# Decoder layer with a routed expert stage: expert results added to the output in memory instead of stored, read back and weighted

## The chip, the cores and the metric

The kernel runs on one core of one Trainium2 chip. The metric is the device time of one execution in microseconds (us). The engines of a core are TensorE (PE), VectorE (DVE), ScalarE (ACT), GpSimd (POOL) and SyncE (SP); 16 DMA engines move data, at the word of SP's queue and of POOL's.

## What is computed

A decoder layer on x of shape 4 x 512 x 512: grouped-query attention, a gated state-space mixer, and a feed-forward part with experts. Only the last matters here:

```
topk_indices, topk_weights = _router(x, router_weight, e_bias)      # 2 of 16 experts per token, weights sum to 1
combine = zeros((T, 16)).at[arange(T)[:, None], topk_indices].add(topk_weights)
h1 = einsum('th,ehi->tei', x, w_up)
a = relu2(h1) * combine[:, :, None]                                  # relu2(v) = relu(v)**2
routed = einsum('tei,eih->th', a, w_down)
shared = relu2(hidden_states @ shared_up) @ shared_down
x = x + routed + shared                                              # hidden_states is the normalized x
```

There are 2048 tokens, so 4096 pairs of a token and an expert. w_up of an expert is 512 x 256, w_down 256 x 512, all in float32.

## The kernel before

All stages stand in one program. Attention and the scan of the mixer take the first 660 us or so. Then `close` (from line 1332) runs the normalizations, the shared feed-forward part and the router; `tiles` (from line 1902) runs the routed experts and ends the kernel. The order of work on each engine is written out by hand, and every engine waits on semaphores.

**Router.** `Router.choose` (line 1186, on DVE) picks two experts a token and their weights, `count` (1164, PE) and `place` (1258, DVE) give each pair a slot. Slots are sorted by expert, each expert beginning on a multiple of 64, and fill 40 tiles of 128 slots. `inverse` (1298, DVE) builds one-hot matrices in bf16 and two planes of numbers (the high and low part of the token), `collect` (1172, PE) multiplies them in 32 matmuls of 80 columns, and `tokens` (1318, DVE) turns the product into two lists: `token_i` (the token of a slot) and `pair_i` (its row in the scratch array `sorted_y`, twice the token plus the choice; an empty slot gets a row out of bounds, which the store skips). Its last instruction raises `s_routed`. PE reaches `collect` between the shared up-projections of batches 2 and 3 (lines 1666 to 1668). POOL then gathers the first two tiles' rows (lines 1503 to 1505) and goes on squaring hidden values of the last batch; SP loads expert weights as rooms come free (lines 1436 to 1466).

**Loop over 40 tiles.** In step i (functions `step` at lines 2005, 2058 and 2100) PE does the up-projection of tile i (line 2017, 16 float32 matmuls in the two halves of the array), the down-projection of tile i-1 (line 2029, 8), two transposes of h of tile i (line 2000), and the four transposes of the input of tile i+2 (line 1990, in `turn_x`). ACT copies the down result of tile i-1 out of PSUM into y (line 2065), then h (2068), then the turned input (2054). DVE does relu and square and copies weights for the second half of the array (2080, 2085). POOL's list is

```
load(2); load(3)
for i in range(40):
    if i + 4 < 40: load(i + 4)      # waits until PE has turned tile i + 2; indirect gather of 128 rows
    store(i)                        # waits for y(i); indirect scatter into sorted_y, with a bound
```

**End.** PE then does the last 24 down-projections of the shared part of batch 3 (line 2043, 6 of 8 terms for each of 4 banks; the first 2 terms were done ahead at line 1615 and added by DVE at line 1824). When the last scatter has landed, SP reads `sorted_y` back in 16 loads (line 1949) into the rooms of the weights; DVE adds the two results of each token, weighted, to `acc`, the residual sum (32 instructions, line 2124), for batch 3 also the PSUM banks (line 2119); SP writes 16 blocks of `acc` to the output (line 1953).

Of the kernel before, what the change touches and what calls it, by code (L numbers as in the profile page):

```python
# [23 lines left out]
P = 128  # L24
# [1055 lines left out]
class Router:  # L1080
# [3 lines left out]
    def __init__(self, nc, ctx, keep, r, room):  # L1084
# [23 lines left out]
        self.m1 = sb("m1", [P, TT])  # L1108
# [24 lines left out]
        self.index = [room[0][:, n * SLOT_TILES:(n + 1) * SLOT_TILES] for n in range(4)]  # L1133
# [10 lines left out]
    def constants(self, pool):  # L1144
        pool.memset(self.before_bf[:, :], 1.0).then_inc(self.s_const, 1)
        pool.wait_ge(self.s_const, 1)

        pool.affine_select(out=self.before_bf[:, :], in_=self.before_bf[:, :], compare_op=ALU.is_ge, fill=0.0, base=-1,
                           pattern=[[1, P]], channel_multiplier=-1).then_inc(self.s_const, 1)
        pool.memset(self.ones_bf[:, :], 1.0).then_inc(self.s_const, 1)  # L1150
        pool.memset(self.ones[:, :], 1.0).then_inc(self.s_const, 1)
        pool.memset(self.base[:, 0, :], 0.0).then_inc(self.s_const, 1)
        for out, pattern, first, per_partition in (
                (self.falling, [[-1, E]], E, 0), (self.unit_start, [[HALF, B * T // HALF]], 0, 0), (self.unit_id, [[1, UNIT_SLOTS]], 0, 0),
                (self.row_id, [[1, P]], 0, 0), (self.tile_row, [[P, SLOT_TILES + 1]], 0, 0),
                (self.token_hi, [[0, 2], [1, B * NT]], 1, 0), (self.token_lo, [[P, 2], [0, B * NT]], 0, 1)):
            pool.iota(out[:, :], pattern, base=first, channel_multiplier=per_partition,
                      allow_small_or_imprecise_dtypes=True).then_inc(self.s_const, 1)
# [13 lines left out]
    def collect(self, pe, out):  # L1172

        pe.wait_ge(self.s_inverse, 1)
        for n in range(2 * B * NT):
            last = pe.matmul(out[:, 0:2 * SLOT_TILES], self.in_row[:, n, :], self.planes[:, n, :, :].rearrange("p w i -> p (w i)"),
                             start=(n == 0), stop=(n == 2 * B * NT - 1))
        last.then_inc(self.s_token, 1)
# [7 lines left out]
    def choose(self, dve):  # L1186
# [52 lines left out]
        for k in range(2):  # L1239

            link(dve.tensor_reduce(m1[:, :], score[:, :, :], AX.X, ALU.max))
            tt(tmp[:, :, :], score[:, :, :], per_tile(m1[:, :]), ALU.is_equal)
            tt(tmp[:, :, :], tmp[:, :, :], per_expert(falling[:, :]), ALU.mult)
            link(dve.tensor_reduce(m1[:, :], tmp[:, :, :], AX.X, ALU.max))
            tt(hot[k], tmp[:, :, :], per_tile(m1[:, :]), ALU.is_equal)
# [10 lines left out]
        dve.tensor_tensor(count_bf[:, :].rearrange("p (t e) -> p t e", e=E), hot[0], hot[1], ALU.add).then_inc(self.s_count, 1)  # L1256

# [40 lines left out]
    def inverse(self, dve):  # L1298
# [15 lines left out]
        for w, token in enumerate((self.token_hi, self.token_lo)):  # L1314
            self.link(dve, dve.tensor_tensor(self.planes[:, :, w, :], self.in_tile[:, :, :], over(token[:, :], NI), ALU.mult))
        dve.tensor_tensor(self.in_row, over(self.row[:, :], P), each(self.row_id[:, :], P), ALU.is_equal).then_inc(self.s_inverse, 1)

    def tokens(self, dve, psum):
        dve.wait_ge(self.s_token, 1)
        hi, lo = psum[:, 0:SLOT_TILES], psum[:, SLOT_TILES:2 * SLOT_TILES]  # L1320
        choice, token, pair, none = self.index
        self.link(dve, dve.tensor_scalar(choice, lo, float(P), None, ALU.is_ge))
        self.link(dve, dve.tensor_scalar(token, hi, float(P), -float(P), ALU.mult, ALU.add))
        self.link(dve, dve.scalar_tensor_tensor(pair, choice, -float(P), lo, ALU.mult, ALU.add))
        self.link(dve, dve.tensor_tensor(token, token, pair, ALU.add))
        self.link(dve, dve.scalar_tensor_tensor(pair, token, 2.0, choice, ALU.mult, ALU.add))
        self.link(dve, dve.tensor_scalar(none, token, 0.0, float(4 * B * T), ALU.is_lt, ALU.mult))
        self.link(dve, dve.tensor_scalar(self.r["token_i"][:, :], token, 0.0, None, ALU.max))
        dve.tensor_tensor(self.r["pair_i"][:, :], pair, none, ALU.add).then_inc(self.r["s_routed"], 1)


def close(nc, d, keep, r):

    ctx = ExitStack()
    with ctx:
# [68 lines left out]

        routed = tiles(nc, d, keep, ctx, r, bank, dve_base, pool_sq, pe_down)
# [3 lines left out]
        def _(sp):  # L1409
# [39 lines left out]
            expert(8)  # L1449
            sp.wait_ge(pe_down.sem, pe_down.upto(4 * 2 - 1))  # L1450
# [3 lines left out]
            expert(11)  # L1454
            sp.wait_ge(r["s_routed"], 1)
# [10 lines left out]
            expert_down(10)  # L1466
            routed["sync"](sp)

        @block.gpsimd
        def _(pool):  # L1470
# [32 lines left out]
            for i in range(2):  # L1503
                pool.indirect_dma_start(out=r["x_first"][:, i, :], out_offset=None, in_=d["norm_rows"],
# [7 lines left out]
        def _(pe):  # L1512
# [88 lines left out]
            def turn_first():  # L1601
                pe.wait_ge(act_relu.sem, act_relu.upto(FK * B - 1))
                pe.wait_ge(r["s_x"][0], 16)
                for k in four:
                    last = pe.transpose(bank[0][:, k * P:(k + 1) * P], r["x_first"][:, 0, k * P:(k + 1) * P], ident[:, :])
# [273 lines left out]
def experts(nc, d, keep):  # L1879

    ctx = ExitStack()
    with ctx:
# [6 lines left out]
            "pair_i": sb([P, SLOT_TILES], U32),  # L1889
# [3 lines left out]
            "x_first": sb([P, 2, D]),  # L1893
            "late": sb([P, LATE]),
            "room": sb,
            "s_x": [ctx.enter_context(nc.semaphore(f"e_x{s}")) for s in range(2)],
# [5 lines left out]
def tiles(nc, d, keep, ctx, r, bank, dve_base, pool_sq, pe_down):  # L1902
# [3 lines left out]
    TT = B * NT  # L1906
    UP = KD * FE

    x_in = [r["x_first"][:, 0, :], r["x_first"][:, 1, :]]
# [6 lines left out]
    y = [keep["attn"][:, 0, s * D:(s + 1) * D] for s in range(2)]  # L1916
    halves = [slice(0, HALF), slice(HALF, P)]

    back = [r["w_all"][:, t, 0:2 * D] for t in range(TT)]
    s_x = r["s_x"]  # L1920
    s_y = [ctx.enter_context(nc.semaphore(f"e_y{s}")) for s in range(2)]
    s_g = [ctx.enter_context(nc.semaphore(f"e_g{s}")) for s in range(TT - 2)] + [keep["s_x"][b].sem for b in (1, 2)]
    before = [0] * (TT - 2) + [keep["s_x"][b].upto(NT) for b in (1, 2)]
    s_o = ctx.enter_context(nc.semaphore("e_out"))
# [10 lines left out]
    pair = Track(nc, ctx, "e_pair", ["first", "second"], 2)  # L1935
    s_late_out, s_late_add = keep["s_late_out"], keep["s_late_add"]
# [8 lines left out]
    def sync(sp):  # L1945
        sp.wait_ge(s_y[0], 16 * (LAST // 2 + 1))
        sp.wait_ge(s_y[1], 16 * ((LAST + 1) // 2))
        for t in range(TT):
            sp.dma_start(back[t], d["sorted_y"][2 * t * P:2 * (t + 1) * P, :].rearrange("(p k) c -> p (k c)", k=2)).then_inc(s_g[t], 16)
        with sp.Fori(0, B) as b:  # L1950
            for t in range(NT):
                pair.wait(sp, b * NT + t, "second")
                sp.dma_start(d["out"][b, t * P:(t + 1) * P, :], keep["acc"][:, b, t * D:(t + 1) * D]).then_inc(s_o, 16)
        sp.wait_ge(s_o, 16 * TT)

    def gpsimd(pool):
# [6 lines left out]
        def store(i):  # L1963
            act_l.wait(pool, i, "y")
            pool.indirect_dma_start(out=d["sorted_y"][0:2 * B * T, :], in_=y[i % 2], in_offset=None, bounds_check=2 * B * T - 1, oob_is_err=False,  # L1965
                                    out_offset=bass.IndirectOffsetOnAxis(ap=r["pair_i"][:, i:i + 1], axis=0))\
                .then_inc(s_y[i % 2], 16)

        load(2)
        load(3)  # L1970
        for i in range(SLOT_TILES):
            if i + 4 < SLOT_TILES:
                load(i + 4)
            store(i)
# [71 lines left out]
    def scalar(act):  # L2046
# [24 lines left out]
        run(step)  # L2071

# [21 lines left out]
    def vector(dve):  # L2094
        dve_m.start(dve)
        pair.start(dve)
# [16 lines left out]

        for t in range(TT):
            dve.wait_ge(s_g[t], before[t] + 16)
            acc = keep["acc"][:, t // NT, (t % NT) * D:(t % NT + 1) * D]
            if t // NT == B - 1:
                dve.wait_ge(s_late_out.sem, s_late_out.upto(t % NT))
                dve.tensor_tensor(acc, bank[t % NT][:, :], acc, ALU.add).then_inc(s_late_add.sem, s_late_add.tick(t % NT))
                dve.wait_ge(s_late_add.sem, s_late_add.upto(t % NT))  # L2120
            for k in range(2):
                if k == 1:
                    pair.wait(dve, t, "first")
                pair.done(dve.scalar_tensor_tensor(acc, back[t][:, k * D:(k + 1) * D], r["weight"][k][:, t:t + 1], acc, ALU.mult, ALU.add),
                          ("first", "second")[k])
# [4 lines left out]
def decoder_layer(nc, d):  # L2130
    with ExitStack() as ctx:
# [21 lines left out]
        keep["s_late_out"], keep["s_late_add"] = Signal(nc, ctx, "late_out"), Signal(nc, ctx, "late_add")  # L2153
# [61 lines left out]
```

## Time and profile before

| | us |
|---|---|
| median of 3 executions (1126.65 to 1132.16) | 1128.84 |
| profiled execution, its time | 1128.89 |
| profiled execution, its span | 1127.2 |
| PE busy in the span | 1060.9 |
| DVE busy | 845.7 |
| POOL busy | 656.7 |

The span runs from the first to the last instruction; the time of the same execution is 1.7 us more. The profile's rows give the start of an instruction or merged group from the span's start, its duration, engine, line of the kernel, operation, what it writes and reads, and in brackets how long the engine had been idle before it and what ended that. The chain of waits follows back from the last instruction what released each step. The windows view sums busy time of each engine in a stretch and gives the granted clock of PE: 1.00 is 2.4 GHz, 0.50 is 1.2 GHz, and a value between them means that part of the stretch ran at either.

### The profile page before, as it was taken

What the parts mean: (1) busy time and instruction counts of PE and PEld (TensorE: products, weight loads), DVE (VectorE), ACT (ScalarE), POOL (GpSimd) and SP (SyncE); (2) the same over time, 40 slices, a digit from 0 to 9 for tenths busy, and PEclk for the clock granted to TensorE, in tenths of its full rate; (3) what the DMA queues carried; (4) which work ended last, traced back from release to release, by engine and by line L of the source; (5) the groups of instructions that cost most, each with busy time, mean ns of one, the idle gap of its engine ahead of it and who ended that gap; (6) DMA issues with size and microseconds to landing.
All of it is one profiled execution on the core that took longest, in us unless ns stands there. A gap on an engine that the chain in (4) does not pass through costs nothing.

```text
span 1127.2 us, 19610 instructions
## 1 busy us (share of the span) xinstructions
PE 1060.9 (94%) x6786; PEld 620.4 (55%) x6786; DVE 845.7 (75%) x1297; ACT 676.8 (60%) x1492; POOL 656.7 (58%) x573
## 2 busy tenths in 40 slices
PE   8999988888999999999989889999999999999993
PEld 3554556666666667666666654544444445555541
DVE  6988699999999999999999989840680045545548
ACT  4876789999999899999999944412011022333310
POOL 2022299999999999999999955202043024444420
PEclk9999989999999999999999999999999999999997
DMA  7210001102111111010221007112225523333329
GB/s 225 94 39 21 21 29 39 37 31 76 34 34 30 39 67 39 30 38 31 84 75 31 20 23 278 38 74 75 75 75 206 167 81 122 122 112 123 108 76 381
DMA packets 50865, 92.95 MB, mean 82 GB/s; under 512 B 9294, under 2 KB 17486, under 8 KB 50768
## 3 DMA queue, kind: packets, MB, share of 16 engines
q1 hardware_dynamic: 44368, 72.82, 19.4%
q0 software_dynamic: 6400, 18.88, 5.2%
q8 instruction: 56, 0.92, 0.3%
q14 instruction: 41, 0.34, 0.1%
HBM read 72.67 MB, written 19.01 MB: 81 GB/s over the span
## 4 chain that ended last, share of the span: by engine, by line
PE 71%; POOL 8%; DVE 7%; ACT 7%; issue 5%; DMA 1%; SPq 0%; DVEq 0%; ACTq 0%; POOLq 0%
PE ps L1570 10%; PE ps L2017 7%; PE ps L2029 6%; PE ps L843 6%; POOL w_all L765 5%; PE ps L1584 5%; PE ps L871 4%; PE ps L358 4%; PE ps L832 4%; PE ps L817 4%; DVE w_all L1042 3%; PE ps L310 3%; PE ps L1593 2%; ACT w_all L956 2%; PE ps L882 2%
## 5 line engine op out<-in xcount | busy, mean ns | idle before, releaser
L765 POOL TENSOR_TENSOR w_all<-w_all 128x512 f32<-128x512 f32 x256 | 320.7, 1272 | 20.1 <-DVE w_all L587 14.8
L1042 DVE TENSOR_TENSOR_SCAN w_all<-ps,w_all 128x512 f32<-128x512 f32 x256 | 298.6, 1205 | 1.2 <-ACT ps L939 0.6
L939 ACT ACTIVATE ps<-w_all,low 128x512 f32<-128x512 f32 x256 | 177.6, 697 | 1.0 <-DVE w_all L1042 0.8
L871 PE MATMUL ps<-ident,w_all 128*128 128x128 f32 x1024 | 162.0, 281 | 9.7 <-DVE acc L1050 9.5
L947 ACT ACTIVATE w_all<-ps,low 128x128 f32<-128x128 f32 (+3 forms) x256 | 132.8, 530 | 13.6 <-DVE low L1034 13.6
L871 PEld LDWEIGHTS ps<-ident,w_all 128*128 128x128 f32 x1024 | 114.9, 142 | 34.7 <-issue 20.8
L956 ACT ACTIVATE w_all<-ps 128x256 f32<-128x256 f32 (+2 forms) x192 | 101.9, 531 | 22.9 <-PE ps L832 22.6
L1034 DVE TENSOR_REDUCE low<-ps 128x2 f32<-128x256 f32 (+3 forms) x128 | 103.8, 811 | 14.6 <-PE ps L817 13.9
L1570 PE MATMUL ps<-w_all 128*128 128x512 f32 x256 | 112.1, 594 | 0.0
L832 PE MATMUL ps<-ident,w_all 128*128 128x128 f32 x640 | 108.8, 285 | 1.5 <-ACT low L1013 1.5
L843 PE MATMUL ps<-w_all,low 128*32 128x128 f32 x1280 | 95.0, 278 | 12.1 <-ACT w_all L956 10.8
L817 PE MATMUL ps<-w_all,attn 32*128 32x384 f32 (+3 forms) x512 | 105.1, 487 | 0.0
L1497 POOL TENSOR_TENSOR w_all<-w_all 128x512 f32<-128x512 f32 x24 | 32.6, 1362 | 123.8 <-ACT w_all L1704 123.8
L832 PEld LDWEIGHTS ps<-ident,w_all 128*128 128x128 f32 x640 | 70.5, 141 | 51.5 <-issue 48.3
L2065 ACT ACTIVATE attn<-ps 128x512 f32<-128x512 f32 x40 | 24.0, 601 | 121.6 <-PE ps L2029 121.6
L773 POOL TENSOR_TENSOR acc<-acc,low 128x512 f32<-128x512 f32 x64 | 81.7, 1277 | 24.6 <-ACT low L968 24.5
L1965 POOL DMA_INDIRECT sorted_y<-attn,low x40 | 40.6, 1015 | 91.3 <-ACT attn L2065 91.3
L1050 DVE SCALAR_TENSOR_TENSOR acc<-ps,low,acc 128x512 f32<-128x512 f32 x128 | 92.7, 724 | 0.0
L843 PEld LDWEIGHTS ps<-w_all,low 128*32 128x32 f32 x1280 | 60.4, 109 | 46.9 <-ACT w_all L956 24.8
L773 POOL TENSOR_TENSOR acc<-acc,w_all 128x512 f32<-128x512 f32 x64 | 81.9, 1280 | 4.0 <-ACT w_all L968 4.0
L1570 PEld LDWEIGHTS ps<-w_all 128*128 128x128 f32 x256 | 47.8, 190 | 58.5 <-issue 56.8
L2017 PE MATMUL ps<-w_all,attn 128*64 x320 | 79.1, 391 | 0.3 <-issue 0.2
(228 smaller groups left out, 1935.2 us busy)
## 6 DMA issues: line engine op xcount, KB each, us to landing
w_all<-b_scratch SPq DMA_DIRECT2D x64, 256.0 KB, 3.2
w_all<-in_w_up SPq DMA_DIRECT2D x16, 512.0 KB, 6.0
w_all<-in_w_down SPq DMA_DIRECT2D x16, 512.0 KB, 7.1
w_all<-sorted_y SPq DMA_DIRECT2D x16, 512.0 KB, 10.5
norms<-attn SPq DMA_DIRECT2D x4, 1024.0 KB, 4.3
out_dram<-acc SPq DMA_DIRECT2D x16, 256.0 KB, 8.8
attn<-in_x SPq DMA_DIRECT2D x3, 1024.0 KB, 6.0
attn<-in_x SPq DMA_DIRECT2D x12, 256.0 KB, 4.3
```

Of the source, the lines that this page charges most:

```text
L765: pool.tensor_tensor(dbu[:, k, :], keep["du"][i // N][:, k * T:(k + 1) * T], b_all[i % 2][:, :], ALU.mult).then_inc(pool_dbu.sem, pool_dbu ...
L773: pool.tensor_tensor(acc, acc, cy[n % 2][:, :], ALU.add).then_inc(pool_acc.sem, pool_acc.tick(n))
L817: last = pe.matmul(sc[:, x, 0:n], keep["attn"][r:r + DH, b, m * T + j * P:m * T + (j + 1) * P], k_4[r:r + DH, b, m // 2, 0:n], start=False ...
L832: last = pe.transpose(tb[:, at:at + P], prob[:, x, off[j] + t * P:off[j] + (t + 1) * P], ident[:, :])
L843: last = pe.matmul(ob[r:r + DH, j * P:(j + 1) * P], keep["v"][:, b * KV + m // 2, t * DH:(t + 1) * DH], prob_t[unit % 2][:, at:at + P], st ...
L871: last = pe.transpose(yb[which][:, k * P:(k + 1) * P], state[i % 2][:, k, t * P:(t + 1) * P], ident[:, :])
L939: act.activation(da[unit % 2][:, :], keep["dt"][i // N][:, k * T:(k + 1) * T], ACT.Exp, scale=keep["a_flat"][:, unit % (N * KD):unit % (N ...
L947: act.activation(prob[:, x, off[j]:off[j] + n], sc[:, x, 0:n], ACT.Exp, bias=neg_max[unit % 2][:, x:x + 1], accum_out=row_sum[unit // 8 % ...
L956: act.activation(prob_t[unit % 2][:, first * n:(first + heads) * n], tb[:, 0:heads * n], ACT.Copy).then_inc(act_turn.sem, act_turn.tick(tu ...
L1042: dve.tensor_tensor_scan(state[i % 2][:, k, :], da[unit % 2][:, :], dbu[:, k, :], 0.0, ALU.mult, ALU.add).then_inc(dve_scan.sem, dve_scan. ...
L1570: last = pe.matmul(bank[m % 2][:, :], s_up[:, k, m * P:(m + 1) * P], norm_t[b][:, k, :], start=(k == 0), stop=(k == 3))
L2017: last = pe.matmul(bank[2 + s][rows, 0:FE], x_t[s][:, k * P + n * HALF:k * P + (n + 1) * HALF], w, start=(k == 0), stop=(k == KD - 1))
```

## The change

The two results of a token are no longer stored, read back and added by DVE. Instead:

- `choose`, `inverse`, `collect` and `tokens` also carry the weight of each slot (in three bf16 pieces, exact in sum) and whether it is that token's lower or higher expert. The lists are now `token_i`, `first_i` (the output row if this is the lower expert, else out of bounds), `second_i` (the reverse) and `w_slot` (the weight).
- ACT's copy of the down result multiplies each slot's row by its weight. y has 4 buffers (before 2), in `acc` of batch 1.
- SP stores `acc` (residual and shared part) to the output per batch, as soon as it is done: batches 0 and 1 during the shared part, 2 and 3 after the last weights.
- POOL adds y to the output's rows with two accumulating indirect scatters a tile, the second after the first has landed.
- x_in has 4 buffers (before 2), in `acc` of batch 0; four tiles are gathered ahead of the loop.
- The end has no read-backs and no DVE work: ACT copies the four late banks of batch 3, POOL adds them to the output by four accumulating DMAs.

```diff
@@ class Router, choose (after the count is released)
+        for k in range(2):
+            tt(late_half[:, k, :], m1[:, k, :], m1[:, 1 - k, :], ALU.is_lt)
+        link(dve.scalar_tensor_tensor(token_lo, late_half[:, :, :], float(P), token_lo, ALU.mult, ALU.add))
+        for k in range(2):
+            link(dve.tensor_copy(rest[:, k, :], weight[k]))
+        flat = rest[:, :, :].rearrange("p k t -> p (k t)")
+        for w in range(3):
+            link(dve.tensor_copy(piece[:, w, :], flat))
+            if w < 2:
+                tt(flat, flat, piece[:, w, :], ALU.subtract)
@@ inverse
+        for w in range(3):
+            self.link(dve, dve.tensor_tensor(self.weights[:, :, w, :], self.in_tile[:, :, :], over(self.piece[:, w, :], NI), ALU.mult))
         dve.tensor_tensor(self.in_row, over(self.row[:, :], P), each(self.row_id[:, :], P), ALU.is_equal).then_inc(self.s_inverse, 1)
@@ collect
+        for n in range(2 * B * NT):
+            last = pe.matmul(out[:, 2 * SLOT_TILES:5 * SLOT_TILES], self.in_row[:, n, :], self.weights[:, n, :, :].rearrange("p w i -> p (w i)"),
                              start=(n == 0), stop=(n == 2 * B * NT - 1))
@@ tokens: 13 instructions where there were 8; the last
+        dve.tensor_tensor(self.r["second_i"][:, :], late_half, row, ALU.add).then_inc(self.r["s_routed"], 1)
@@ close, SP
+            def store(b):
+                sp.wait_ge(dve_base.sem, dve_base.upto(4 * b + 3))
+                if b > 0:
+                    sp.wait_ge(s_out.sem, s_out.upto(b - 1))
+                sp.dma_start(d["out"][b, :, :].rearrange("(t p) c -> p t c", p=P),
+                             keep["acc"][:, b, :].rearrange("p (t c) -> p t c", c=D)).then_inc(s_out.sem, s_out.tick(b))
             expert(8)
+            store(0)
...
             expert(11)
+            store(1)
             sp.wait_ge(r["s_routed"], 1)
...
             expert_down(10)
+            store(2)
+            store(3)
@@ close, POOL
-            for i in range(2):
-                pool.indirect_dma_start(out=r["x_first"][:, i, :], out_offset=None, in_=d["norm_rows"],
+            pool.wait_ge(s_out.sem, s_out.upto(0))
+            for i in range(4):
+                pool.indirect_dma_start(out=r["x_in"][i], out_offset=None, in_=d["norm_rows"],
@@ tiles, SP: the whole of sync is now
+        sp.wait_ge(s_sum, 16 * NT)
@@ tiles, POOL
-        def store(i):
+        def add_first(i):
             act_l.wait(pool, i, "y")
+            pool.indirect_dma_start(out=out_rows, in_=y[i % YB], in_offset=None, bounds_check=B * T - 1, oob_is_err=False, compute_op=ALU.add,
+                                    out_offset=bass.IndirectOffsetOnAxis(ap=r["first_i"][:, i:i + 1], axis=0))\
+                .then_inc(s_first[i % 2], 16)
+
+        def add_second(i):
+            pool.wait_ge(s_first[i % 2], 16 * (i // 2 + 1))
+            pool.indirect_dma_start(out=out_rows, in_=y[i % YB], in_offset=None, bounds_check=B * T - 1, oob_is_err=False, compute_op=ALU.add,
+                                    out_offset=bass.IndirectOffsetOnAxis(ap=r["second_i"][:, i:i + 1], axis=0))\
+                .then_inc(s_second[i % YB], 16)
-        load(2)
-        load(3)
+        pool.wait_ge(s_out.sem, s_out.upto(B - 1))
         for i in range(SLOT_TILES):
-            if i + 4 < SLOT_TILES:
-                load(i + 4)
-            store(i)
+            add_first(i)
+            if i > 0:
+                add_second(i - 1)
+            if i + XB < SLOT_TILES:
+                load(i + XB)
+        add_second(LAST)
+        for s in range(YB):
+            pool.wait_ge(s_second[s], 16 * ((LAST - s) // YB + 1))
+        for t in range(NT):
+            pool.wait_ge(s_late_copy.sem, s_late_copy.upto(t))
+            pool.dma_start(d["out"][B - 1, t * P:(t + 1) * P, :], late[t], accum_op=ALU.add).then_inc(s_sum, 16)
+        pool.wait_ge(s_sum, 16 * NT)
@@ tiles, ACT
-                if i >= 3:
-                    act.wait_ge(s_y[s1], (i - 1) // 2 * 16)
-                act_l.done(act.activation(y[s1], bank[6 + s1][:, :], ACT.Copy), "y")
+                if i == 1:
+                    act.wait_ge(s_out.sem, s_out.upto(1))
+                if i - 1 >= YB:
+                    act.wait_ge(s_second[(i - 1) % YB], (i - 1) // YB * 16)
+                act_l.done(act.activation(y[(i - 1) % YB], bank[6 + s1][:, :], ACT.Copy, scale=r["w_slot"][:, i - 1:i]), "y")
...
+        act.wait_ge(s_out.sem, s_out.upto(B - 1))
+        for t in range(NT):
+            act.wait_ge(s_late_out.sem, s_late_out.upto(t))
+            act.activation(late[t], bank[t][:, :], ACT.Copy).then_inc(s_late_copy.sem, s_late_copy.tick(t))
@@ tiles, DVE: the loop over 16 blocks after the steps (lines 2114 to 2125) is gone
```

## Rows read from the trace of the kernel before

**Rows 1.** The page: busy us, share of the span and instructions of each engine.
```profile
PE 1060.9 (94%) x6786; PEld 620.4 (55%) x6786; DVE 845.7 (75%) x1297; ACT 676.8 (60%) x1492; POOL 656.7 (58%) x573
```

**Rows 2.** Windows: length, busy us of PE, PEld, DVE, ACT, POOL, clock, DMA, GB/s.
```profile
919.20:1082.40 163.20, 163.18 (x1114) 84.18 (x1113) 84.49 (x222) 51.80 (x112) 71.77 (x72) 1.00 0.33 109
```

**Rows 3.** Timeline, one step of the tile loop: ACT, PE, POOL.
```profile
1002.75 0.60 ACT L2065 ACTIVATE attn<-ps 128x512 f32<-128x512 f32 x1 [3.00 <-PE ps L2029]
1003.52 0.42 PE L2017 MATMUL ps<-w_all,attn 128*64 x1
...
1004.15 1.02 POOL L1965 DMA_INDIRECT sorted_y<-attn,low  x1 [2.10 <-ACT attn L2065]
1005.47 0.98 POOL L1959 DMA_INDIRECT low<-norms,low  x1 [0.30 <-issue]
1007.23 0.60 ACT L2065 ACTIVATE attn<-ps 128x512 f32<-128x512 f32 x1 [3.08 <-PE ps L2029]
1007.39 0.60 PE L1990 MATMUL ps<-ident,low 128*128 128x128 f32 x4
```

**Rows 4.** Chain of waits, the first steps of the loop: start, us, what.
```profile
909.48 3.34 DMA low<-norms,low
912.86 0.66 PE ps L1990 x4
913.75 3.42 PE ps L2017 x16
917.16 1.94 PE ps L2029 x8
...
924.31 1.88 PE ps L2017 x16
926.18 1.72 PE ps L2029 x8
...
1078.46 1.88 PE ps L2017 x16
```

**Rows 5.** One line's view, L1965 (ns min/median/max; landing), and timeline of the first gathers.
```profile
L1965 POOL DMA_INDIRECT sorted_y<-attn,low x40: 982/1017/1030, 920.6 to 1090.4; - x40
DMA to landing us min/median/max: 2.1/2.8/3.1
848.06 0.20 DVE L1329 TENSOR_TENSOR low<-w_all 128x40 uint32<-128x40 f32 x1
848.56 1.16 POOL L1504 DMA_INDIRECT low<-norms,low  x1 [1.53 <-DVE low L1329]
```

**Rows 6.** Timeline, the end of the kernel.
```profile
1107.07 2.74 PE L2043 MATMUL ps<-attn,low 128*128 128x512 f32 x6
```

**Rows 7.** Stores of 1 MB in the page; timeline of DVE's last add.
```profile
norms<-attn SPq DMA_DIRECT2D x4, 1024.0 KB, 4.3
908.77 0.69 DVE L1824 TENSOR_TENSOR acc<-ps,acc 128x512 f32<-128x512 f32 x1 [1.03 <-PE ps L1615]
```

**Rows 8.** The router: chain on PE, and DVE instructions beside it.
```profile
845.27 1.15 PE ps L1176 x32
873.96 27.47 PE ps L1593 x64
838.89 4.42 DVE L1316 TENSOR_TENSOR w_all<-low 128x4096 bf16<-128x4096 f32 x1
L1315 DVE TENSOR_TENSOR w_all<-w_all,low x2: 1491/1851/2211, 835.1 to 836.6; 128x1280 bf16<-128x1280 f32 x2
817.63 0.69 DVE L1824 TENSOR_TENSOR acc<-ps,acc 128x512 f32<-128x512 f32 x1 [5.82 <-PE ps L1584]
```

**Rows 9.** Windows around PE's idle stretches, columns as in Rows 2.
```profile
140.00:155.00 15.00, 10.53 (x45) 5.61 (x44) 12.88 (x16) 10.89 (x27) 14.06 (x12) 0.70 0.08 27
660.00:665.00 5.00, 2.98 (x51) 1.86 (x49) 4.72 (x5) 3.38 (x6) 4.94 (x5) 1.00 0.01 3
910.00:915.00 5.00, 3.40 (x24) 1.90 (x22) 2.28 (x6) 0.98 (x2) 2.36 (x3) 0.91 0.40 108
```

More of the change, by code:

```diff
@@ L1107, in __init__ @@
         self.g = g[:, 0:8 * TT * GR].rearrange("p (n t g) -> p n t g", n=8, g=GR)
-        self.m1 = sb("m1", [P, TT])
+        spare = room[1][:, 2 * TT * SLOT_TILES:]
+        self.m1 = spare[:, 0:2 * TT].rearrange("p (k t) -> p k t", k=2)
+        self.late_half = spare[:, 2 * TT:4 * TT].rearrange("p (k t) -> p k t", k=2)
+        self.rest = spare[:, 4 * TT:6 * TT].rearrange("p (k t) -> p k t", k=2)
+        self.piece = spare[:, 6 * TT:9 * TT].bitcast(BF16).rearrange("p (w q) -> p w q", w=3)
         self.den = sb("den", [P, TT])
@@ L1132, in __init__ @@
         self.planes = room[3].bitcast(BF16)[:, 0:PAIRS * 2 * SLOT_TILES].rearrange("p (n w i) -> p n w i", n=PAIRS, w=2)
-        self.index = [room[0][:, n * SLOT_TILES:(n + 1) * SLOT_TILES] for n in range(4)]
+        self.weights = room[0].bitcast(BF16)[:, 0:PAIRS * 3 * SLOT_TILES].rearrange("p (n w i) -> p n w i", n=PAIRS, w=3)
+        self.index = [room[0][:, n * SLOT_TILES:(n + 1) * SLOT_TILES] for n in range(5)]
         self.s_bias = ctx.enter_context(nc.semaphore("d_bias"))
@@ L1155, in constants @@
                 (self.row_id, [[1, P]], 0, 0), (self.tile_row, [[P, SLOT_TILES + 1]], 0, 0),
-                (self.token_hi, [[0, 2], [1, B * NT]], 1, 0), (self.token_lo, [[P, 2], [0, B * NT]], 0, 1)):
+                (self.token_hi, [[0, 2], [1, B * NT]], 1, 0), (self.token_lo, [[0, 2], [0, B * NT]], 0, 1)):
             pool.iota(out[:, :], pattern, base=first, channel_multiplier=per_partition,
@@ L1175, in collect @@
         for n in range(2 * B * NT):
-            last = pe.matmul(out[:, 0:2 * SLOT_TILES], self.in_row[:, n, :], self.planes[:, n, :, :].rearrange("p w i -> p (w i)"),
+            pe.matmul(out[:, 0:2 * SLOT_TILES], self.in_row[:, n, :], self.planes[:, n, :, :].rearrange("p w i -> p (w i)"),
+                      start=(n == 0), stop=(n == 2 * B * NT - 1))
+        for n in range(2 * B * NT):
+            last = pe.matmul(out[:, 2 * SLOT_TILES:5 * SLOT_TILES], self.in_row[:, n, :], self.weights[:, n, :, :].rearrange("p w i -> p (w i)"),
                              start=(n == 0), stop=(n == 2 * B * NT - 1))
@@ L1239, in choose @@
         for k in range(2):
-            link(dve.tensor_reduce(m1[:, :], score[:, :, :], AX.X, ALU.max))
-            tt(tmp[:, :, :], score[:, :, :], per_tile(m1[:, :]), ALU.is_equal)
+            link(dve.tensor_reduce(m1[:, k, :], score[:, :, :], AX.X, ALU.max))
+            tt(tmp[:, :, :], score[:, :, :], per_tile(m1[:, k, :]), ALU.is_equal)
             tt(tmp[:, :, :], tmp[:, :, :], per_expert(falling[:, :]), ALU.mult)
-            link(dve.tensor_reduce(m1[:, :], tmp[:, :, :], AX.X, ALU.max))
-            tt(hot[k], tmp[:, :, :], per_tile(m1[:, :]), ALU.is_equal)
+            link(dve.tensor_reduce(m1[:, k, :], tmp[:, :, :], AX.X, ALU.max))
+            tt(hot[k], tmp[:, :, :], per_tile(m1[:, k, :]), ALU.is_equal)
             if k == 0:
@@ L1256, in choose @@
         dve.tensor_tensor(count_bf[:, :].rearrange("p (t e) -> p t e", e=E), hot[0], hot[1], ALU.add).then_inc(self.s_count, 1)
+        late_half, rest, piece = self.late_half, self.rest, self.piece
+        token_lo = self.token_lo[:, :].rearrange("p (k t) -> p k t", k=2)
+        for k in range(2):
[8 more added lines that the diff above has]
+                tt(flat, flat, piece[:, w, :], ALU.subtract)
     def place(self, dve, psum_before, psum_all):
@@ L1320, in tokens @@
         hi, lo = psum[:, 0:SLOT_TILES], psum[:, SLOT_TILES:2 * SLOT_TILES]
-        choice, token, pair, none = self.index
-        self.link(dve, dve.tensor_scalar(choice, lo, float(P), None, ALU.is_ge))
+        piece = [psum[:, (2 + w) * SLOT_TILES:(3 + w) * SLOT_TILES] for w in range(3)]
+        late_half, token, row, none, share = self.index
+        w_slot, away = self.r["w_slot"][:, :], float(2 * B * T)
+        self.link(dve, dve.tensor_copy(share, piece[2]))
+        self.link(dve, dve.tensor_tensor(share, share, piece[1], ALU.add))
+        self.link(dve, dve.tensor_tensor(w_slot, share, piece[0], ALU.add))
+        self.link(dve, dve.tensor_scalar(late_half, lo, float(P), None, ALU.is_ge))
         self.link(dve, dve.tensor_scalar(token, hi, float(P), -float(P), ALU.mult, ALU.add))
[L1324 to L1327, printed above, removed]
+        self.link(dve, dve.scalar_tensor_tensor(row, late_half, -float(P), lo, ALU.mult, ALU.add))
+        self.link(dve, dve.tensor_tensor(token, token, row, ALU.add))
+        self.link(dve, dve.tensor_scalar(none, token, 0.0, 4 * away, ALU.is_lt, ALU.mult))
+        self.link(dve, dve.tensor_tensor(row, token, none, ALU.add))
         self.link(dve, dve.tensor_scalar(self.r["token_i"][:, :], token, 0.0, None, ALU.max))
-        dve.tensor_tensor(self.r["pair_i"][:, :], pair, none, ALU.add).then_inc(self.r["s_routed"], 1)
+        self.link(dve, dve.scalar_tensor_tensor(self.r["first_i"][:, :], late_half, away, row, ALU.mult, ALU.add))
+        self.link(dve, dve.tensor_scalar(late_half, late_half, -away, away, ALU.mult, ALU.add))
+        dve.tensor_tensor(self.r["second_i"][:, :], late_half, row, ALU.add).then_inc(self.r["s_routed"], 1)
 def close(nc, d, keep, r):
@@ L1403, in down_bank @@
             return bank[2 + t % 2 + 4 * (t // 2)] if b > 0 else bank[2 + t % 2]
+        s_out = r["s_out"]
         routed = tiles(nc, d, keep, ctx, r, bank, dve_base, pool_sq, pe_down)
@@ L1604, in turn_first @@
                 for k in four:
-                    last = pe.transpose(bank[0][:, k * P:(k + 1) * P], r["x_first"][:, 0, k * P:(k + 1) * P], ident[:, :])
+                    last = pe.transpose(bank[0][:, k * P:(k + 1) * P], r["x_in"][0][:, k * P:(k + 1) * P], ident[:, :])
                 last.then_inc(pe_late.sem, pe_late.tick(2))
@@ L1888, in experts @@
             "token_i": sb([P, SLOT_TILES], U32),
-            "pair_i": sb([P, SLOT_TILES], U32),
+            "first_i": sb([P, SLOT_TILES], U32),
+            "second_i": sb([P, SLOT_TILES], U32),
+            "w_slot": sb([P, SLOT_TILES]),
             "s_w_up": ctx.enter_context(nc.semaphore("d_weights_up")),
@@ L1892, in experts @@
             "s_routed": ctx.enter_context(nc.semaphore("d_routed")),
-            "x_first": sb([P, 2, D]),
+            "hole": sb([P, 2 * D - 2 * SLOT_TILES]),
+            "x_in": [keep["acc"][:, 0, s * D:(s + 1) * D] for s in range(4)],
+            "s_out": Signal(nc, ctx, "out_in", 16),
             "late": sb([P, LATE]),
             "room": sb,
-            "s_x": [ctx.enter_context(nc.semaphore(f"e_x{s}")) for s in range(2)],
+            "s_x": [ctx.enter_context(nc.semaphore(f"e_x{s}")) for s in range(4)],
         }
@@ L1905, in tiles @@
     FK = FE // P
-    TT = B * NT
     UP = KD * FE
-    x_in = [r["x_first"][:, 0, :], r["x_first"][:, 1, :]]
+    x_in = r["x_in"]
     XB = len(x_in)
@@ L1915, in tiles @@
     h_t = keep["logits"][:, :, :].rearrange("p b n -> p (b n)")
-    y = [keep["attn"][:, 0, s * D:(s + 1) * D] for s in range(2)]
+    YB = 4
+    y = [keep["acc"][:, 1, s * D:(s + 1) * D] for s in range(YB)]
+    late = [keep["acc"][:, B - 1, t * D:(t + 1) * D] for t in range(NT)]
+    out_rows = d["out"].rearrange("b t c -> (b t) c")
     halves = [slice(0, HALF), slice(HALF, P)]
[L1919 to L1924, printed above, removed]
+    s_x, s_out = r["s_x"], r["s_out"]
+    s_first = [ctx.enter_context(nc.semaphore(f"e_first{s}")) for s in range(2)]
+    s_second = [ctx.enter_context(nc.semaphore(f"e_second{s}")) for s in range(YB)]
+    s_sum = ctx.enter_context(nc.semaphore("e_sum"))
     pe_m = Track(nc, ctx, "e_pe_main", ["up"], 2)
@@ L1934, in tiles @@
     dve_d = Track(nc, ctx, "e_dve_down", ["down0", "down1"])
-    pair = Track(nc, ctx, "e_pair", ["first", "second"], 2)
-    s_late_out, s_late_add = keep["s_late_out"], keep["s_late_add"]
+    s_late_out, s_late_copy = keep["s_late_out"], keep["s_late_copy"]
     FK_S = FS // P
@@ L1945, in sync @@
     def sync(sp):
[L1946 to L1954, printed above, removed]
+        sp.wait_ge(s_sum, 16 * NT)
     def gpsimd(pool):
@@ L2095, in vector @@
         dve_m.start(dve)
-        pair.start(dve)
         dve.wait_ge(r["s_w_down"], 16 * E)
@@ L2112, in vector @@
         run(step)
[L2114 to L2125, printed above, removed]
     return {"sync": sync, "gpsimd": gpsimd, "tensor": tensor, "scalar": scalar, "vector": vector, "first_weights": first_weights}
@@ L2152, in decoder_layer @@
         keep["s_settle"], keep["s_settle_pe"] = Signal(nc, ctx, "settle"), Signal(nc, ctx, "settle_pe")
-        keep["s_late_out"], keep["s_late_add"] = Signal(nc, ctx, "late_out"), Signal(nc, ctx, "late_add")
+        keep["s_late_out"], keep["s_late_copy"] = Signal(nc, ctx, "late_out"), Signal(nc, ctx, "late_copy")
         keep["low"] = sb("low", [P, LOW])[:, :]
```

3 lines of the change are left out of this document (removed).

## The prediction

> **What bounds the kernel now.** I read the page first: PE is busy 1060.9 of the span's 1127.2 us [rows 1], so the kernel ends when PE's work ends, plus whatever stands behind it. Then the windows: from 919.2 to 1082.4 us, the loop over tiles, PE is busy 163.18 of 163.20 us at full clock, POOL 71.77 [rows 2]. What DVE, SP and the DMA engines do behind PE's last matmul is the end, 17 us. So the change can win there; in the loop it can only lose, by making something late for PE.
>
> The timeline shows the loop's rhythm. From one copy of y to the next are 4.48 us there [rows 3]; between the up-projections at 924.31 and 1078.46 lie 35 steps, 4.40 each [rows 4]. POOL's scatter starts 0.80 us after ACT's copy of y ends (1003.35 to 1004.15), takes 1.02; the gather follows 0.30 after it and takes 0.98 [rows 3]. How long a gather takes to land stands in the chain: 3.34 us from its start until PE goes on [rows 4]. The scatters land 2.1 to 3.1 us after their start [rows 5].
>
> **The end: a gain of 12.6 us.** Gone are 16 read-backs, 36 DVE instructions and 16 stores behind PE. The last late matmul ends at 1109.81 [rows 6], 17.4 us before the span does. After it, in the changed kernel: ACT's copy, 0.6 us like the copy of y; 0.8 us to POOL; an accumulating DMA of 256 KB, for which I take the gather's 3.34. That ends at 1114.6 instead of 1127.2. Bounds for that DMA: 2.1 us (shortest scatter) and twice 3.34, so the gain is 9 to 14. The earlier three closing DMAs run under PE's matmuls, 5 us each bank. That the stores of `acc` (4 MB) now run earlier costs nothing by my reading: their cover is PE's busy shared part. The last goes out after DVE's last add (909.46), takes 4.3 us as the norms' stores of 1 MB do, and the first scatter comes at 920.6, 6.8 us after that [rows 5, 7]. If that cover went, the first scatter would wait for a store, 4.3 us at most, once.
>
> **The router: a loss of 5.4 us.** `inverse` gets three more products of 128 x 1280, 1.85 us each, so s_inverse comes at 843.31 + 5.55 = 848.9 (end of L1316 plus three of L1315). PE wanted it at 845.27 [rows 8]: 3.6 us of waiting. `collect` gets 32 matmuls of 120 columns; 32 of 80 take 1.15, so 1.7 more. The dozen small instructions in `choose` come after the count is released and before DVE's 5.82 us of idle, which hides them: at 0.20 us as L1329's they are under 3 us [rows 5, 8]. Those in `tokens`, 5 more, make s_routed another 1.2 us later. Behind it stand SP's weight loads for the experts, wanted over 50 us later (the loop begins at 909), and POOL's gathers, now four (2.6 us more), with the last batch's squares queued behind them; PE needs those only after its 27.47 us on batch 2, from 873.96 [rows 8]. Free, then; without that cover, 11 us. SP's stores 0 and 1 take their place in its queue ahead of such loads and are as well covered. Bounds for the router: 2 (were the products quick) to 8.
>
> **The loop: a loss of 61.2 us.** This step decides. POOL now has three DMAs a tile, and the order matters: the gather for tile i+4 stands behind add_first(i) and add_second(i-1). Before, it stood ahead of the scatter of y(i). When is it wanted? y(i)'s copy ends at 1003.35, and PE comes to the turn of tile i+4 at 1007.39 [rows 3]: 4.04 us later. When is it there? 0.80 to POOL; 1.02 for the first scatter; then the second. Its distance is not shown: at least 0.30, as between scatter and gather, at most 0.80, which is what a scatter takes after its wait even when POOL was long idle, while a gather takes 0.30 in both situations (the first one follows DVE's last result at 848.26 by that) [rows 3, 5]. That suggests that the preparation of a bounded scatter isn't overlapped, so I take 0.77. Then 1.02, 0.30, and 3.34 to land: 7.25 in all. So the input is 3.2 us late.
>
> Does this repeat? The input landed, PE turns it (0.04 and 0.60) and y two tiles on is copied 3.71 + 0.60 us later (1003.52 to 1007.83) [rows 3, 4]: 4.95. So y(i) to y(i+2) takes 7.25 + 4.95 = 12.20 us through POOL and the gather, against 2 x 4.40 = 8.80 of PE's own work. PE will idle some 3 us on every second tile and little on the other (POOL itself needs 4.9 us a tile). The gathers inside the loop are 36, in two interleaved chains of 18 rounds: 18 x 3.40 = 61.2 us. Bounds for a round: 2.1 us for landing and 0.30 between scatters give 10.49 (18 x 1.69 = 30.4 us); scatters at twice 1.02 give 14.24 (18 x 5.44 = 97.9). The wait of add_second(i-1) costs nothing in any of these: the scatter that it waits for began a tile earlier, over 6 us, and lands in 3. Should accumulation take over twice as long to land, the gather queued behind it on POOL would be late by as much again. ACT's wait for y's buffer looks four tiles back and is met. The weighting is free: the copy has the same shape.
>
> The Trainium skill, "DMA: Bandwidth & Descriptors", section "Anatomy of one DMA — SWDGE (gpsimd) path", gives 2.0 us plus bytes/436e3 for a transfer of POOL's queue. For 256 KB an estimate by it is 2.6 us where the row shows 3.34; if that held the loop would lose 48 us instead of 61. The row decides.
>
> **PE's clock: a loss of 17.6 us.** After 1.6 us of idle between 910 and 915 the clock fell to 1.2 GHz, and the next up- and down-projection took 3.42 + 1.94 instead of 1.88 + 1.72: 1.76 us [rows 4, 9]. After 4.5 us of idle between 140 and 155 it fell for half of that stretch or more (mean 0.70); after 2.0 between 660 and 665 it stayed at 2.4 GHz [rows 9]. So an idle stretch of 3 us sometimes costs 1.76, and in the loop that lies in the round. I take half of the 18 rounds (15.8 us; bounds 0 and 31.7) and one fall at the router (1.8).
>
> **Sum**, against the profiled execution: 1127.2 - 12.6 + 5.4 + 61.2 + 17.6 = 1198.8, and 1.7 between span and time: 1200.5 us. The profiled execution, 1128.89, is the median of the three, so nothing is to be shifted.
>
> **Rivals.**
> (a) The round is shorter: gathers land in 2.1 us and scatters follow at 0.30, no clock falls. Then 1127.2 - 12.6 + 5.4 + 30.4 + 1.7 = 1152.1. For it: the scatters' landing, median 2.8. Against: the one gather that the chain shows. Everything up to 1184 (my sum without clock falls) I count here: 0.28.
> (b) Accumulating scatters cost POOL twice the time: 1127.2 - 12.6 + 5.4 + 97.9 + 17.6 + 1.7 = 1237.2. For it: nothing in the trace prices accumulation. "Collectives: The Full Stack", section "The bandwidth ceiling: the fold count and why AG ≠ RS ≠ AR", in the Trainium skill says that an add emits two read descriptors a chunk where a copy emits one, because it reads two operands; this rule speaks against the change, and no run here shows it yet. Chance 0.15.
> (c) Faster: a scatter in which half the rows are out of bounds is cheap on POOL. If each took 0.35 us with 0.30 between them, and gathers landed in 2.1, y's copy to landing is 4.2 us, PE is hardly held up, and 1127.2 - 12.6 + 5.4 + 1.7 = 1121.7 plus a few tenths. It decides from 4.04 us down. Against: the 40 scatters, whose numbers of skipped slots differ, all took 0.98 to 1.03 [rows 5]. Chance 0.05.
> (d) Gains and losses meet near zero: the same with scatters of 0.5 us. 0.02.
> (e) The forecast, 1184 to 1217: 0.50.
> That the change doesn't do what it says, with read-backs still at the end, is excluded by the diff.
>
> **The numbers.** The range 1158 to 1235 leaves out the shortest rounds, (c) and (d) below and most of (b) above. A measurement of this kernel tells about 0.5% (5.6 us) from no change. Faster 0.05, same 0.02, slower 0.93.
>
> **What would show it.** In the changed profile: PE busy in the loop falls to about 70 to 75%, with "DMA <-norms" as releaser of line 1990's transposes on every second tile, some 3 us each; POOL shows three indirect DMAs a tile of 1.0 us; the clock row of the loop lies between 0.5 and 1; `collect` begins 3.6 us later after up(2); after the last matmul 5 us are left. It is wrong if PE stays over 98% busy in the loop, or if what PE waits for is not a gather.

## The result, and the profile after

The changed kernel takes 1260.28 us (median of 4, 1258.29 to 1263.27) against 1129.03 before (4 executions): ratio 1.116, 95% interval [1.113, 1.120]. It is slower by 131 us, where 72 were forecast; the range ended at 1235. The profiled execution has a span of 1257.9 us.

The page's first rows, as [rows 1]:

```profile
span 1257.9 us, 19659 instructions
PE 1109.8 (88%) x6818; PEld 641.8 (51%) x6818; DVE 831.8 (66%) x1279; ACT 683.5 (54%) x1496; POOL 751.2 (60%) x617
```

The windows view of the loop, with the columns of [rows 2]:

```profile
927.00:1211.00 284.00, 198.29 (x1052) 97.39 (x1051) 82.59 (x211) 52.68 (x107) 151.18 (x107) 0.82 0.37 63
```

PE, busy all the time before, is busy for 70% of the loop, at a mean granted clock of 0.82. The waits of that stretch (engine, line, releaser: total us, times, longest) name one wait above all for PE:

```profile
PE ps L2042 <- DMA acc<-norms,low: 83.2, 18, 5.8
```

L2042 is the turn of an input tile (its four transposes), `acc<-norms` its gather. It waits 18 times, once per round of two tiles, 4.6 us on the average. One round in the chain of waits (start, us, what), to be read against [rows 3, 4]; L2069 is the up-projection, L2081 the down-projection, L2119 the copy of y, L2003 and L2009 the two scatters:

```profile
1060.43 1.12 PE ps L2042 x4
1061.55 3.61 PE ps L2069 x16
1065.16 1.94 PE ps L2081 x8
1067.10 0.03 issue
1067.12 0.69 ACT acc L2119
...
1068.38 0.03 POOLq L2009
...
1068.59 1.57 POOL out_dram L2003
1070.15 0.30 issue
1070.46 1.80 POOL out_dram L2009
1072.26 0.31 issue
1072.57 3.89 DMA acc<-norms,low
```

The chain goes turn, up, down, copy of y, first scatter, second scatter, gather, and back to the turn: 16.1 us for two tiles (1060.43 to 1076.51). The copies of y of tiles 2 and 36 start at 940.52 and 1216.88, so a round took 16.26 us on the average.

Where the 131 us stand, by the starts of ACT's copies of y in both traces: the first y is 7.1 us later (919.74 to 926.81, end of copy), the 39 tiles from there to the last y take 302.2 instead of 169.9, which is 132.3 more, and the stretch after the last y takes 28.9 instead of 37.5, which is 8.6 less. The router's part of the first term, in the chain:

```profile
850.62 2.31 PE ps L1181 x32
852.93 2.15 PE ps L1184 x32
855.09 27.52 PE ps L1613 x64
```

PE starts `collect` (L1181, L1184) at 850.62 instead of 845.27, after 4.18 us of idle, and its first 32 matmuls take 2.31 us instead of 1.15: the mean granted clock between 850.6 and 855.0 is 0.64. Batch 3's projection starts 8.7 us later than in [rows 8]. Some of that is made up before the first y.

### The profile page after: what moved, and what is told of

Same layout as the page of the kernel before. It is cut to its first block, busy times and chain, and to the rows that moved or that the text cites. A ratio compares the mean times of both kernels' runs of the same rounds, so it can differ in the third digit from the quotient of the medians.

```text
span 1257.9 us, 19659 instructions
## 1 busy us (share of the span) xinstructions
PE 1109.8 (88%) x6818; PEld 641.8 (51%) x6818; DVE 831.8 (66%) x1279; ACT 683.5 (54%) x1496; POOL 751.2 (60%) x617
## 3 DMA queue, kind: packets, MB, share of 16 engines
q0 software_dynamic: 15296, 19.98, 9.3%
## 4 chain that ended last, share of the span: by engine, by line
PE 62%; DVE 9%; ACT 8%; POOL 8%; issue 6%; DMA 6%; POOLq 0%; DVEq 0%; SPq 0%; ACTq 0%
PE ps L1613 7%; PE ps L843 6%; DMA acc<-norms,low 6%; PE ps L2069 6%; PE ps L871 4%; PE ps L1627 4%; PE ps L832 4%; PE ps L817 4%; PE ps L358 4%; DVE w_all L1042 4%; PE ps L2081 4%; PE ps L310 2%; POOL out_dram L2009 2%; ACT w_all L956 2%; POOL out_dram L2003 2%
## 5 line engine op out<-in xcount | busy, mean ns | idle before, releaser
L2003 POOL DMA_INDIRECT out_dram<-acc,low x40 | 62.9, 1572 | 163.1 <-ACT acc L2119 155.3
L2162 DVE TENSOR_SCALAR low<-ps 128x256 f32<-128x256 f32 x40 | 17.0, 424 | 194.0 <-PE ps L2069 194.0
L2119 ACT ACTIVATE acc<-ps,low 128x512 f32<-128x512 f32 x40 | 27.5, 688 | 156.9 <-PE ps L2081 145.1
L2069 PE MATMUL ps<-w_all,attn 128*64 x320 | 105.5, 488 | 3.2 <-issue 2.4
L843 PE MATMUL ps<-w_all,low 128*32 128x128 f32 x1280 | 95.0, 278 | 12.3 <-ACT w_all L956 11.1
L2069 PE MATMUL ps<-attn 128*64 128x256 f32 x320 | 105.5, 488 | 0.0
L2042 PE MATMUL ps<-ident,acc 128*128 128x128 f32 x156 | 31.8, 340 | 83.2 <-DMA acc<-norms,low 83.2
```

The source lines that it names most:

```text
L843: last = pe.matmul(ob[r:r + DH, j * P:(j + 1) * P], keep["v"][:, b * KV + m // 2, t * DH:(t + 1) * DH], prob_t[unit % 2][:, at:at + P], st ...
L2069: last = pe.matmul(bank[2 + s][rows, 0:FE], x_t[s][:, k * P + n * HALF:k * P + (n + 1) * HALF], w, start=(k == 0), stop=(k == KD - 1))
```

## The experiments

Seven further kernels ran, each beside the kernel before on the same chip (1129.3 us in the first series, 1129.9 in the second).

**Gather first** (e1), the changed kernel with POOL's order turned:

```diff
         for i in range(SLOT_TILES):
+            if i + XB < SLOT_TILES:
+                load(i + XB)
             add_first(i)
             if i > 0:
                 add_second(i - 1)
-            if i + XB < SLOT_TILES:
-                load(i + XB)
```

> The changed kernel with POOL's order turned: in iteration i first the gather of tile i+4, then the two accumulating scatters. Theory A (the gather stands behind the scatters and lands too late for PE): PE's long stalls go, the loop is then bound by POOL's own three DMAs, 0.30 + 1.01 + 0.30 + 1.57 + 0.30 + 1.57 = 5.05 us a tile where the changed kernel has 7.75; 39 tiles x 2.7 = 105 us less, some 1155 us, and the clock stays at full. Theory B (accumulation itself fills the rings or memory, so whatever is queued comes late): the tile stays above 7 us and the time above 1200 us.

Measured: 1157.7 us, ratio 1.025 [1.024, 1.027]. Moving one line gives back 102.6 of the 131 us. From the first copy of y (925.55) to the last (1122.95) are 39 x 5.06 us, which is POOL's own work. In the windows view of the loop:

```profile
930.00:1090.00 160.00, 142.50 (x930) 71.48 (x929) 74.91 (x187) 47.04 (x93) 130.90 (x93) 1.00 0.58 100
```

The clock is full though PE still idles 11% of the time, in short pieces. POOL's timeline has no pause but the 0.30 us between DMAs:

```profile
1002.74 1.02 POOL L1997 DMA_INDIRECT acc<-norms,low  x1 [0.31 <-issue]
1004.06 1.68 POOL L2003 DMA_INDIRECT out_dram<-acc,low  x1 [0.30 <-issue]
1006.04 1.72 POOL L2009 DMA_INDIRECT out_dram<-acc,low  x1 [0.30 <-issue]
1008.06 1.02 POOL L1997 DMA_INDIRECT acc<-norms,low  x1 [0.30 <-issue]
```

Theory B falls: with accumulation in the same amount, but the gather ahead of it, the whole change costs 28 us and not 131.

**Plain scatter** (e2), the changed kernel without `compute_op=ALU.add` in both scatters.

> The changed kernel with compute_op left out of both scatters: rows are overwritten instead of added to, so the sums are missing. Theory A (an accumulating descriptor is what costs): POOL's scatters fall from 1.57 to about 1.02 us, the gathers behind them land in 3.3 instead of 4.0, a round of two tiles takes 14.4 instead of 16.26 us, 18 rounds give about 33 us, 1227 us. Theory B (the half of rows that is out of bounds, or the output tensor, makes them dearer): 1.57 us stays and so does 1260.

Measured: 1206.4 us, ratio 1.068 [1.059, 1.077], 54 less than the changed kernel, more than the 33 expected. That is the middle of two executions that lie 17 us apart: 1214.86 with a mean granted clock of 0.967 over the whole execution (the profiled one) and 1197.99 with 0.985. The views of lines 2003, 2009 and 1997 (ns min/median/max), and the landing of 1997's gathers:

```profile
L2003 POOL DMA_INDIRECT out_dram<-acc,low x40: 984/1007/1030, 928.0 to 1187.1; - x40
L2009 POOL DMA_INDIRECT out_dram<-acc,low x40: 982/987/999, 933.6 to 1190.0; - x40
...
DMA to landing us min/median/max: 3.2/3.4/4.4
```

With the addition the same lines read:

```profile
L2003 POOL DMA_INDIRECT out_dram<-acc,low x40: 1553/1571/1638, 927.8 to 1231.6; - x40
L2009 POOL DMA_INDIRECT out_dram<-acc,low x40: 1553/1572/1816, 933.9 to 1235.3; - x40
...
DMA to landing us min/median/max: 3.3/4.0/5.4
```

So addition costs POOL 0.56 us a scatter. The number of rows that are out of bounds costs or saves nothing: 1.00 us for a plain scatter of about half a tile here, 1.02 for a whole one before [rows 5]. POOL's queue moves 15296 packets with the addition and 10176 without, 64 more for each of the 80 scatters, for the same 20 MB. This agrees in kind with what "Collectives: The Full Stack" of the Trainium skill says, in its section "The bandwidth ceiling: the fold count and why AG ≠ RS ≠ AR", of two read descriptors an add; in size it is a factor of 1.56 on POOL's time, not 2.

The medians of the landing, 4.0 and 3.4 us, are not the price of the addition alone. In the changed kernel's chain the gathers take 3.32 to 3.48 us in seven of the first eight rounds, as without the addition, and 3.88 to 5.04 in the last ten:

```profile
1041.63 3.32 DMA acc<-norms,low
1171.17 5.04 DMA acc<-norms,low
```

They grow late in the loop without any addition too: 3.31 to 4.18 from 1038 on in this run, and up to 4.82 in the run e4 below, against 3.2 to 3.8 earlier in the loop. What makes them grow is open.

In the profiled execution a round takes 13.9 us instead of the expected 14.4, and PE's stalls are shorter (52.1 us in 19 waits, 2.7 each). The mean clock between 930 and 1090 is 0.88 instead of 0.83. What is gained over the 33 us goes with the clock: the execution with the higher clock is the faster one by 17 us.

**PE kept busy** (e3, 16 matmuls; e5, 8), the changed kernel with useless work ahead of the wait:

```diff
             if ahead:
+                if i >= 2 and i % 2 == 0:
+                    for k in range(WARM):
+                        pe.matmul(bank[s][:, 0:FE], ident[:, :], r["w_all"][:, 0, 0:FE], start=True, stop=True)
                 turn_x(i + 2)
```

> The changed kernel with 16 useless float32 matmuls of 256 columns (3.4 us at full clock) into a free bank in every even step, just before PE waits for the late gather. Theory A (the clock falls in PE's stalls, and the slowed projections stand in the round): clock 0.95 or more in the loop, turn, up and down take 4.2 instead of 6.7 us, 18 x 2.5 = 45 us less, some 1215 us. Theory B (the fall costs nothing since PE has slack): no change or slower, 1260 or more.

Measured: 1253.9 us, ratio 1.110. A miss in size: the trace has two records for each of these float32 matmuls, 32 a round, and they took 6.91 us instead of 3.4, so that PE itself became the bound; in the loop's window it is busy without a gap, at full clock:

```profile
930.00:1090.00 160.00, 160.00 (x946) 107.58 (x944) 48.02 (x124) 31.55 (x63) 84.65 (x60) 1.00 0.38 64
```

Even so, 124 us of useless work in the loop (18 x 6.91) did not make the kernel slower; it is 6 us faster, in two executions. With 8 the test is clean.

> As the run before with useless matmuls, but 8 in place of 16: the 16 took 6.9 us a round, twice what was meant, and made PE itself the bound (8.8 + 6.9 = 15.7 us a round, busy all the time). 8 take 3.5 us, less than PE idles. Theory A (each fall of the clock stands in the round with 2.5 us): the clock stays at 2.4 GHz, a round takes 13.8 instead of 16.3 us, 18 x 2.5 = 45 us less than the changed kernel, some 1215 us. Theory B (the falls cost nothing): 1260. Theory C (the 1.5 us of idle left still let the clock fall): between them.

Measured: 1224.1 us, ratio 1.083 [1.081, 1.086]: 36 us less than the changed kernel, with nothing but more work for PE.

```profile
930.00:1090.00 160.00, 150.11 (x907) 90.49 (x906) 55.21 (x142) 36.45 (x71) 98.86 (x71) 1.00 0.43 76
```

The copies of tiles 2 and 36 start at 941.55 and 1177.73: a round of 13.9 us, where 13.8 was expected. Theory A stands; the first y came 3 us later than in the changed kernel, which explains a part of the 9 us between 1224 and the expected 1215.

**The kernel before, gather last** (e4), no accumulation anywhere:

```diff
         for i in range(SLOT_TILES):
-            if i + 4 < SLOT_TILES:
-                load(i + 4)
             store(i)
+            if i + 4 < SLOT_TILES:
+                load(i + 4)
```

> The kernel before, with only POOL's two DMAs of an iteration exchanged: the scatter of y(i), then the gather of tile i+4. No accumulation, no other change. Theory A: from the end of y's copy 0.8 + 1.02 + 0.30 + 3.3 to 4.0 = 5.4 to 6.1 us until the input has landed, wanted after 4.04; a round takes 10.4 to 11.1 us against 8.8, 29 to 41 us more, 1158 to 1170 us; if the clock falls in each round as well, some 1200. Theory B (only accumulation matters): 1129 us.

Measured: 1173.9 us, ratio 1.039 [1.037, 1.041]: 45 us for the exchange of two lines. The round in its chain of waits:

```profile
984.90 3.34 DMA low<-norms,low
988.24 0.04 issue
988.28 0.66 PE ps L1990 x4
988.94 0.21 issue
989.14 1.95 PE ps L2017 x16
991.09 1.74 PE ps L2029 x8
992.83 0.02 issue
992.85 0.61 ACT attn L2065
...
994.25 1.01 POOL sorted_y L1965
995.26 0.30 issue
995.57 3.34 DMA low<-norms,low
```

From gather to gather 10.67 us; the working on record had 10.4 to 11.1. PE's stalls are about 1 us here (25.6 us in 26 waits) and the clock mostly stays up, with a mean of 0.98 between 930 and 1090. In four late rounds the up-projection takes 2.99 to 3.63 us instead of 1.95, some 6 us in all, about what stands above 1170.

**Deeper buffers** (e6) and a **later collect** (e7). e6 is e1 with x_in in 8 buffers (`acc` of batches 0 and 1, all gathered ahead of the loop), y in 8 (batches 2 and 3), the late banks in batch 0's room, and the waits on `s_out` that follow from it. e7 adds:

```diff
-            router.collect(pe, bank[5])
-            up(3, 0, 8)
+            up(3, 0, 2)
+            router.collect(pe, bank[5])
+            up(3, 2, 8)
```

> Gather first, with 8 input buffers (all 8 gathered ahead of the loop, in POOL's idle time) and 8 buffers for y, late banks in batch 0's room. Theory A (with the order mended, what is left of the loss is POOL's work, 80 scatters of 1.57 + 0.30 and 32 gathers of 1.31, 191.5 us from the first y at 927, which deep buffers let run on under PE's last 24 matmuls): scatters end at 1118, landing and four closing DMAs until 1134, time some 1136 us; PE's loop itself goes at near 4.4 us a tile. Theory B (something in PE's loop other than inputs and y buffers holds it, such as a slow landing): the loop stays at 5 us a tile, 1155 us.

> As the run with 8 and 8 buffers, and PE does two of the eight up-projections of batch 3 before the router's collect instead of after it, so that the three new products of the weights on DVE are hidden. Theory A (PE waited 5.35 us for them and the clock fell): the start of batch 3's first projection is no later than before plus the 32 new matmuls, 5 to 6 us less than the run beside it, some 1130 us. Theory B (POOL, started later by the router, sets the end anyway): 0 to 2 us less.

Measured: 1145.6 us, ratio 1.013 [1.012, 1.015], and 1138.9 us, ratio 1.008 [1.006, 1.009]. In e6 PE copies the first 28 y at 4.40 to 4.8 us a tile. POOL falls behind by some 0.65 us a tile meanwhile, and then PE waits for inputs again: the gather issued at 1044.64 lands 5.49 us later, and PE turns its tile at 1050.17. From there on the loop goes at POOL's pace: 179.2 us from first to last y against 169.9 before. No wait for a y buffer shows. The end has no slack left: POOL's scatters end at 1128.9, their landing, four closing DMAs and the last landing follow. Expected were 1136; the first y came 3 us later than assumed, and many scatters took 1.7 us instead of 1.57 (their medians are still 1.57). In e7 `collect` costs only its own time:

```profile
854.42 1.15 PE ps L1181 x32
855.57 1.68 PE ps L1184 x32
857.25 20.66 PE ps L1615 x48
```

The expected 5 to 6 us came as 6.8, so the router's cost was mostly PE's wait and the fall of the clock in it. Neither version beats the kernel before: POOL's 80 accumulating scatters are 150 us at 1.57 + 0.30, and with 32 gathers 191, more than PE's 176.

## Why the prediction was wrong

What failed is the size of a round: forecast at 12.20 us and 0.88 more for the clock (15.8 in 18 rounds), it took 16.26. The terms follow.

**Right: the mechanism.** "the gather for tile i+4 stands behind add_first(i) and add_second(i-1)" and lands too late, on every second tile, in 18 rounds. The waits show 18, and e1 and e4 show it from both sides: the order alone is worth 102.6 us in the changed kernel and costs 45 us in the old one.

**Wrong: the price of a scatter.** The step took 1.02 us a scatter from the copying one and kept twice that as a bound. It is 1.57 (e2: 1.00 without the addition), and 1.80 for the second in the round shown. Against the 2.04 in the sum that is 1.3 us a round, 24 us in 18.

**Wrong: the distance between scatters.** I took 0.77 us, reading scatter and gather after their waits as a sign that preparation isn't overlapped. It is 0.30. In the round shown POOL's queue comes to the second scatter at 1068.38, 0.21 us before the row of the first begins, so the second isn't held up by a wait of its own. That gives 0.5 us a round back, 9 us in 18.

**Wrong: the landing of the gather.** 3.34 us was taken from one gather ahead of the loop. In the chain's 18 rounds it is 3.94 on the average: 0.6 a round, 11 us. Most of that stands in the last ten rounds, and the addition is at most a part of its cause (see e2).

**Wrong: PE's clock, with the scatters the largest miss.** The forecast had a fall in half of the rounds at 1.76 us. The clock fell in all 18. The up-projection after the stall, 1.88 us at full clock, takes 3.61 to 3.68 in 13 of them in the chain and 2.86 to 3.14 in 5:

```profile
1029.01 1.12 PE ps L2042 x4
1030.31 3.68 PE ps L2069 x16
1044.99 1.11 PE ps L2042 x4
1046.15 3.01 PE ps L2069 x16
```

With the turn and the down-projection, a whole fall is 1.12 + 3.61 + 1.94 = 6.7 us instead of 4.2, so 2.5; the short ones are some 1.6. 13 x 2.5 + 5 x 1.6 = 40 us instead of 15.8; e5 measures 36 us net. Each fall was dearer because the turn is slow as well: it took 0.66 us behind the one gather that [rows 4] shows, and 1.12 here. The falls were more frequent, and the longer stall is the likely reason: 4.6 us on the average where some 3 were reckoned, because the other terms were too small. At the 2.7 us of e2 one execution had a mean clock of 0.967, with 17 of its 18 up-projections slowed, and the other 0.985; in the changed kernel all four lie between 0.945 and 0.951.

Together 24 - 9 + 11 + 25 = 51 us, and 1.6 for the copy of y: the forecast called the weighting free, but the copy takes 0.69 us instead of 0.60. The loop missed by 55 (132.3 against 61.2 + 15.8), nearly the whole error of the forecast, which is 60.

**The end**, 8.6 instead of 12.6 us: PE's part behind the last y is as reckoned, but the last closing DMA is issued at 1250.00, 0.9 us after PE's last matmul, and the span ends 7.9 us after that, where 3.34 were taken. The longest landing of the four is 5.3; what the remaining 2.6 are is open.

**The router**, 5.4 + 1.8 forecast, and PE is 8.7 us later behind it. PE idled 4.18 us in front of `collect` instead of 3.6, for the three products took 6.05 us instead of 5.55. The 64 matmuls of `collect` took 4.46 us instead of 1.15, of which 1.7 was reckoned and 1.6 is the fallen clock (e7 has them at 2.83). The other 1.2 us were there before: PE began the up-projections of batch 2 at 818.80 instead of 817.64, and DVE was as late; why is open. The 5.35 us that e7's expectation calls waiting are the idle time and this shift. Of the 8.7, 7.1 reached the first y.

**The rivals.** (b), dearer accumulation, was right in kind, and its factor 2 would have given the measured time to 23 us by too large a price and too rare a fall of the clock. (a) and (c) fall with the landing and scatter rows. The Trainium skill's 2.0 us plus bytes over 436e3 ("DMA: Bandwidth & Descriptors", section "Anatomy of one DMA — SWDGE (gpsimd) path"), an estimate of 2.6 us, is too short for this gather: 3.2 us was the shortest in the views of its line (e2, e5).

## What to carry to other kernels

On an engine that issues DMAs in order, the prefetch goes ahead of anything that waits for a result: one line's place was worth 103 us here. Before replacing a store and a read-back by accumulating scatters, count their issue time per tile against the bound engine's work per tile: here 5.05 against 4.40 us, so even well ordered the loop could not keep its pace, and a tail of 17 us could not pay for it. A long stall of PE in every round costs more than its length: behind 4.6 us of idle on the average the matmuls ran at 1.2 GHz, for which e5 gives a price of 36 us, while behind stalls of about 1 us (e4) the clock mostly stayed at 2.4 GHz.

## What was not expected of the hardware

- Useless matmuls in front of a wait made the kernel 36 us faster (e5), and even 124 us of them did not make it slower (e3).
- An accumulating indirect scatter takes POOL 1.57 us where a plain one takes 1.00, with the same rows, about half of them out of bounds, and 64 packets more.
- The same gather took 3.3 us to land early in the loop and up to 5.0 late in it, and it grew without accumulation too (e2, e4).
- Scatters of the same form took 1.55 to 1.88 us within one kernel (e6). The long ones in the round shown run beside DVE's copies of weights; whether those are the cause was not tried.
- The clock stayed at 2.4 GHz with PE idle for 11% of the loop in short pieces (e1) and had a mean of 0.82 with PE idle for 30% in pieces of up to 5.8 us (the changed kernel).
